# Local attention on one Trainium2 core: scores of even and odd heads in two PSUM banks, turned q and turned k in one

## The reference

```python
qkv = shift_tokens(x) @ Wqkv            # 128 -> 3 x 1024: 16 heads of 64
q = l2norm(q) * qs;  k = l2norm(k) * ksc
q = q * cos * scale + rotate_half(q) * sin * scale
k = k * cos / scale + rotate_half(k) * sin / scale
# windows of 32 queries; each sees its own and the previous 32 keys
sim = einsum('bhwie,bhwje->bhwij', bq, bk2) * 8.0
attn = softmax(where(mask, -big, sim))
x = einsum('bhwij,bhwje->bhwie', attn, bv2) @ Wo + x
x = (a * gelu(gate)) @ W2 + b2 + x      # a, gate from layernorm(shift_tokens(x)) @ W1 + b1
```

## Time and profile before

| | |
|---|---|
| median of 3 runs | 4349.73 us (4349.69 to 4349.89) |
| profiled execution, its own time | 4352.31 us |
| its span, first to last instruction | 4350.3 us |
| mean granted TensorE clock | 0.972 of full speed |
| the two local blocks, about | 365 to 1990 us and 2250 to 3870 us |
| a step without feed-forward work | 6.83 us |
| the step with the Gelu | 10.90 us |

### The profile page before, as it was taken

One profiled execution on the slowest core, in us unless ns is written; L12 is line 12 of the kernel. 1 busy time (PEld: TensorE's weight loads), 2 busy tenths in 40 slices (PEclk: granted clock), 3 DMA queues, 4 the chain that ended last, 5 costly groups with the idle time before them and its releaser, 6 DMA issues. The chain is left out here.

```text
span 4350.3 us, 128583 instructions
## 1 busy us (share of the span) xinstructions
PE 4059.4 (93%) x53847; PEld 2018.4 (46%) x53847; DVE 3351.9 (77%) x5020; ACT 2912.0 (67%) x7325; POOL 2388.5 (55%) x1684
## 2 busy tenths in 40 slices
PE   5998999999999999998989999999999999987897
PEld 3223555555455555553435555555554554543442
DVE  3776888888888888884758888888888888864673
ACT  2765777777777777774657777777777777754564
POOL 3314766666666666663226766666666666631220
PEclk7999999999999999997999999999999999999998
DMA  4221000000000000002220000000000000000110
GB/s 166 57 60 31 2 22 7 2 22 7 21 7 2 22 7 2 2 2 60 62 65 2 4 25 2 21 7 14 14 2 21 7 2 2 2 10 31 41 51 10
DMA packets 68917, 97.79 MB, mean 22 GB/s; under 512 B 34472, under 2 KB 58756, under 8 KB 62340
## 3 DMA queue, kind: packets, MB, share of 16 engines
q1 hardware_dynamic: 67476, 83.28, 6.5%
q10 hardware_dynamic: 864, 6.29, 0.4%
HBM read 72.18 MB, written 16.78 MB: 20 GB/s over the span
## 5 line engine op out<-in xcount | busy, mean ns | idle before, releaser
L402 POOL TENSOR_TENSOR ra<-ra,rb 128x1024 f32<-128x1024 f32 x384 | 927.2, 2415 | 330.2 <-DVE rb L741 330.1
L416 POOL TENSOR_TENSOR qkr<-ra,inv 128x1024 f32<-128x1024 f32 x384 | 731.0, 1904 | 608.2 <-ACT inv L680 604.5
L448 PE MATMUL ps<-wvo,xs 128*32 128x512 f32 x6144 | 821.2, 607 | 72.3 <-ACT vs L602 72.3
L493 PE MATMUL ps<-wq,xs 128*128 128x512 f32 x1536 | 747.8, 609 | 6.2 <-DVE rb L741 3.6
L653 ACT ACTIVATE pr<-ps,neg 128x64 f32<-128x64 f32 x3072 | 668.0, 337 | 7.1 <-DVE neg L718 7.1
L602 ACT ACTIVATE vs<-ps 128x512 f32<-128x512 f32 x768 | 450.8, 587 | 226.6 <-PE ps L448 225.3
L515 PEld LDWEIGHTS ps<-kt,qt 64*32 64x32 f32 x24576 | 360.3, 107 | 294.0 <-issue 290.3
L718 DVE TENSOR_REDUCE neg<-ps 128x8 f32<-128x512 f32 x384 | 263.7, 687 | 279.4 <-PE ps L515 272.5
L493 PEld LDWEIGHTS ps<-wq,xs 128*128 128x128 f32 x1536 | 274.0, 191 | 431.1 <-issue 334.0
L738 DVE TENSOR_TENSOR ra<-ps,rope 128x1024 f32<-128x1024 f32 x384 | 451.8, 1177 | 24.4 <-ACT sq L627 17.3
L1502 DVE TENSOR_REDUCE nm<-ps 128x1 f32<-128x512 f32 (+3 forms) x768 | 379.2, 550 | 116.9 <-PE ps L1267 114.4
(11 more groups left out here) (251 smaller groups left out, 6199.0 us busy)
## 6 DMA issues: line engine op xcount, KB each, us to landing
wq<-in_L_ffn_Wqkv SPq DMA_DIRECT2D x12, 1024.0 KB, 5.2
wvo<-wvo_scratch SPq DMA_DIRECT2D x12, 1024.0 KB, 4.9
wvo_scratch<-pt ACTq DMA_DIRECT2D x6, 1024.0 KB, 4.0
w<-in_L_ffn_W SPq DMA_DIRECT2D x12, 341.0 KB
qs<-norm_pieces SPq DMA_DIRECT2D x9, 384.0 KB
ks<-norm_pieces SPq DMA_DIRECT2D x9, 384.0 KB
qs<-latent_pieces SPq DMA_DIRECT2D x9, 384.0 KB
ks<-latent_pieces SPq DMA_DIRECT2D x9, 384.0 KB
```

What stands on the lines that cost most here:

```text
L402: pool.tensor_tensor(ra[:, m % 2, :, :], ra[:, m % 2, :, :], rb[:, :, :], ALU.add).then_inc(sum_done.sem, 1)
L416: pool.tensor_tensor(qkr[:, m % 2, :, :].rearrange("p s (h c) -> p (s h) c", c=HD), ra[:, m % 2, :, :].rearrange("p s (h c) -> p (s h) c", ...
L448: last = pe.matmul(VP[32 * j:32 * j + 32, :], xs[:, turn % 2, v * WIN:v * WIN + WIN], wvo[l % 2][:, j, :], start=True, stop=True)
L493: last = pe.matmul(PJ[:, qk, :], xs[:, turn % 2, t * P:t * P + P], wq[l % 2][:, at:at + 512], start=True, stop=True)
```

## The change

Four things change together.

1. Banks. SB becomes the first 256 columns of banks 3 and 4: even heads write bank 3, odd heads bank 4. Turned q and turned k share bank 2 (`TURN`). Eight consecutive products now use four strips of output partitions and both halves of the rows.
2. TensorE's order: turned q stands before the output product, turned k where both stood. Turned k waits for the copy of turned q, turned q for the copy of the previous turned k.
3. ScalarE copies turned q before the eight Exp. VectorE clamps the sum of squares before it copies turned k and adds the attention residual.
4. The heads come in another order within an item, and the preparation of the value weights (L1355 and the two copies behind it) follows.

The diff, without the lines that only rename indices in the preparation:

```diff
-    PJ, TQ, TK, SB, VP, PO, FB = ps[:, 0:2, :], ps[:, 2, :], ps[:, 3, :], ps[:, 4, :], ps[:, 5, :], ps[:, 6, :], ps[:, 7, :]
+    PJ, TURN, SB, VP, PO, FB = ps[:, 0:2, :], ps[:, 2, :], ps[:, 3:5, 0:TB * KEYS], ps[:, 5, :], ps[:, 6, :], ps[:, 7, :]
...
-                for i in range(2):
-                    for w in range(TB):
-                        for j in range(4):
-                            p, e = divmod(j, 2)
+                for w in range(TB):
+                    for pair in range(4):
+                        for e in range(2):
                             rows = slice(64 * e, 64 * e + 64)
-                            at = (i * TB + w) * KEYS
-                            last = pe.matmul(SB[32 * j:32 * j + 32, at:at + KEYS], qt[rows, m % 2, (2 * i + p) * TB + w, :],
-                                             kt[rows, 4 * up + 2 * i + p, t * P + w * WIN:t * P + w * WIN + KEYS], start=False, stop=i == 1 and w == TB - 1, skip_group_check=True)
+                            last = pe.matmul(SB[32 * pair:32 * pair + 32, e, w * KEYS:w * KEYS + KEYS], qt[rows, m % 2, pair * TB + w, :],
+                                             kt[rows, 4 * up + pair, t * P + w * WIN:t * P + w * WIN + KEYS], start=False, stop=w == TB - 1, skip_group_check=True)
...
+            m = item(k, LAG_TR)
+            if m is not None:
+                pe.wait_ge(qkr_done.sem, qkr_done.at(m + 1))
+                pe.wait_ge(k_kept.sem, k_kept.at(m))
+                for j in range(4):
+                    last = pe.transpose(TURN[:, j * P:j * P + P], qkr[:, m % 2, 0, j * P:j * P + P], core.ident[:, :])
+                last.then_inc(tq_ready.sem, 1)
             m = item(k, LAG_AV)
...
             m = item(k, LAG_TR)
             if m is not None:
-                pe.wait_ge(qkr_done.sem, qkr_done.at(m + 1))
-                pe.wait_ge(q_kept.sem, q_kept.at(m))
+                pe.wait_ge(q_kept.sem, q_kept.at(m + 1))
                 for j in range(4):
-                    last = pe.transpose(TQ[:, j * P:j * P + P], qkr[:, m % 2, 0, j * P:j * P + P], core.ident[:, :])
-                last.then_inc(tq_ready.sem, 1)
-                pe.wait_ge(k_kept.sem, k_kept.at(m))
-                for j in range(4):
-                    last = pe.transpose(TK[:, j * P:j * P + P], qkr[:, m % 2, 1, j * P:j * P + P], core.ident[:, :])
+                    last = pe.transpose(TURN[:, j * P:j * P + P], qkr[:, m % 2, 1, j * P:j * P + P], core.ident[:, :])
                 last.then_inc(tk_ready.sem, 1)
...
+            m = item(k, LAG_TR)
+            if m is not None:
+                act.wait_ge(tq_ready.sem, tq_ready.at(m + 1))
+                act.activation(qt[:, m % 2, :, :].rearrange("p w c -> p (w c)"), TURN, ACT.Copy).then_inc(q_kept.sem, 1)
             m = item(k, LAG_S)
...
-            m = item(k, LAG_TR)
-            if m is not None:
-                act.wait_ge(tq_ready.sem, tq_ready.at(m + 1))
-                act.activation(qt[:, m % 2, :, :].rearrange("p w c -> p (w c)"), TQ, ACT.Copy).then_inc(q_kept.sem, 1)
...
+            m = item(k, 0)
+            if m is not None:
+                dve.wait_ge(ss_done.sem, ss_done.at(m + 1))
+                dve.tensor_scalar(ssq[:, m % 2, :], ssq[:, m % 2, :], 1e-24, None, ALU.max).then_inc(ssc_done.sem, 1)
             m = item(k, LAG_TR)
             if m is not None:
                 dve.wait_ge(tk_ready.sem, tk_ready.at(m + 1))
...
-            m = item(k, 0)
-            if m is not None:
-                dve.wait_ge(ss_done.sem, ss_done.at(m + 1))
-                dve.tensor_scalar(ssq[:, m % 2, :], ssq[:, m % 2, :], 1e-24, None, ALU.max).then_inc(ssc_done.sem, 1)
```

More of the change, by code:

```diff
@@ L502, in tensor @@
                     pe.wait_ge(tables_done.sem, tables_done.at(1))
-                    pe.matmul(SB.rearrange("p (i c) -> p i c", i=2), core.ident16[:, :], band[:, None, :].to_broadcast([P, 2, TB * KEYS]),
-                              start=True, stop=False, skip_group_check=True)
+                    for e in range(2):
+                        pe.matmul(SB[:, e, :], core.ident16[:, :], band[:, :], start=True, stop=False, skip_group_check=True)
                 else:
@@ L652, in scalar @@
                 for n in range(8):
-                    last = act.activation(pr[:, m % 2, n, :], SB[:, n * KEYS:n * KEYS + KEYS], ACT.Exp, bias=neg[:, m % 2, n:n + 1])
+                    last = act.activation(pr[:, m % 2, n, :], SB[:, n // TB, n % TB * KEYS:n % TB * KEYS + KEYS], ACT.Exp, bias=neg[:, m % 2, n:n + 1])
                 last.then_inc(exp_done.sem, 1)
             before = m
-            m = item(k, LAG_TR)
-            if m is not None:
-                act.wait_ge(tq_ready.sem, tq_ready.at(m + 1))
-                act.activation(qt[:, m % 2, :, :].rearrange("p w c -> p (w c)"), TQ, ACT.Copy).then_inc(q_kept.sem, 1)
             if before is not None and before + 1 < STEPS:
@@ L662, in scalar @@
                 act.wait_ge(exp_done.sem, exp_done.at(before + 1))
-                act.activation(SB.rearrange("p (i c) -> p i c", i=2), bandf[:, kind, None, :].to_broadcast([P, 2, TB * KEYS]), ACT.Copy).then_inc(band_set.sem, 1)
+                act.activation(SB, bandf[:, kind, None, :].to_broadcast([P, 2, TB * KEYS]), ACT.Copy).then_inc(band_set.sem, 1)
             m = item(k, 0)
@@ L717, in vector @@
                 dve.wait_ge(s_ready.sem, s_ready.at(m + 1))
-                dve.tensor_reduce(neg[:, m % 2, :], SB.rearrange("p (n c) -> p n c", c=KEYS), AX.X, ALU.max, negate=True).then_inc(max_done.sem, 1)
+                dve.tensor_reduce(neg[:, m % 2, :].rearrange("p (e w) -> p e w", e=2), SB.rearrange("p e (w c) -> p e w c", c=KEYS), AX.X, ALU.max, negate=True).then_inc(max_done.sem, 1)
             m = item(k, LAG_PN)
@@ L771, in vector @@
                 t, up = divmod(m % STEPS_A_TURN, 2)
-                dve.tensor_copy(kt[:, 4 * up:4 * up + 4, WIN + t * P:WIN + t * P + P], TK.rearrange("p (k c) -> p k c", k=4)).then_inc(k_kept.sem, 1)
+                dve.tensor_copy(kt[:, 4 * up:4 * up + 4, WIN + t * P:WIN + t * P + P], TURN.rearrange("p (k c) -> p k c", k=4)).then_inc(k_kept.sem, 1)
             if (a := ff_turn(k, 3)) is not None:
@@ L984, in small_attention @@
         wvo = [pt[:, i, :].rearrange("p (j c) -> p j c", j=4) for i in range(2)]
+        by_unit = lambda a: a.rearrange("p j (u c) -> p u j c", u=4)
         wvt = [out[:, 2 * i:2 * i + 2, :].rearrange("p g (k c) -> p (g k) c", c=P) for i in range(2)]
@@ L1352, in tensor @@
                     for e in range(2):
-                        u, j = divmod(2 * c + e, 4)
+                        u, j = 2 * (c // 4) + e, c % 4
                         rows = slice(64 * e, 64 * e + 64)
-                        last = pe.matmul(ps[:, 2 + j, u * P:u * P + P], wvt[l % 2][rows, c, :], wo[l][rows, c, :], start=True, stop=True)
+                        last = pe.matmul(ps[:, 2 + u, j * P:j * P + P], wvt[l % 2][rows, c, :], wo[l][rows, c, :], start=True, stop=True)
                 last.then_inc(vw_mm.sem, 1)
@@ L1541, in vector @@
                     dve.wait_ge(vw_stored[l % 2].sem, vw_stored[l % 2].at(16 * (l // 2)))
-                dve.tensor_copy(wvo[l % 2][:, 2:4, :], ps[:, 4:6, :]).then_inc(vw_kept_dve.sem, 1)
+                dve.tensor_copy(by_unit(wvo[l % 2])[:, 2:4, :, :], ps[:, 4:6, :].rearrange("p u (j c) -> p u j c", j=4)).then_inc(vw_kept_dve.sem, 1)
             yield
```

2 lines of the change are left out of this document (1 added, 1 removed).

## The result

The changed kernel took 4493.95 us (median of 4 runs, 4491.43 to 4497.39) against 4349.81 for the kernel before in the same session: a ratio of 1.0324, 95% interval 1.0311 to 1.0336. The profiled execution spans 4495.4 us, 145 more than the 4350.3 of before. Of these 145, 142 lie in the two local blocks: counted from the first to the last score burst of each, they last 1595.9 and 1590.5 us before and 1666.5 and 1661.6 after.

A forecast was written before the change was run, and what follows sets the result against it. TensorE, busy 93%, was taken as the bound. Turns +87 us (46 of +1.90), first turns +6, tables +20, clock +17: +130 on 4350.3, 4480, less 2.6 about 4478 us; forecast 4430 to 4520 (0.58), range 4375 to 4560.

The forecast's parts named there:

- The score burst: TensorE's score products at each step's start: eight tiles at a time instead of four, a gain of 0.42 us.
- the mean step: Feed-forward step with the mean product, one per turn of eight steps: 0.42 us shorter, 7.60 us.
- the three other feed-forward steps: Feed-forward steps besides those with W2, mean product and Gelu: 0.14 us shorter each, 0.42 us a turn.
- the plain step: Step without feed-forward work: the next score burst waits for the k copy, 7.00 us instead of 6.83.
- Clamp, k copy, burst: VectorE's clamp held until GpSimd's addition ends, k copy behind it, next score burst waiting: plain step 7.00 us, not 6.69.
- Turned q and L416: TensorE's turned q waits for GpSimd's product: 0.70 us in the W2 step (10.40), 1.36 in the next (8.05).
- The Gelu step: Step where ScalarE computes the Gelu: turned k waits for the q copy, 11.70 us instead of 10.90.
- First turns and tables: Each block's first turn without feed-forward work, +6 us; ten times two table products delaying the k copy, +20 us.
- The clock: Ten more falls of the granted clock behind idle stretches of TensorE, 1.7 us each: +17 us.
- The faster rival: TensorE stays the bound, clamp not held or k copy on time, L416 ready: 4290 us, chance 0.13.
- No eight tiles: The score burst stays 1.03 us and only the costs stay: 4555 us, chance 0.10.
- part of what it says: Waits half as long as worked out, Gelu step as forecast: +0.9 us a turn, 4400 us, chance 0.15.

The follow-up runs named there:

- e1_clamp_alone: Kernel before, with only VectorE's clamp moved ahead of the copy of turned k: 4413.89 us, ratio 1.0133.
- e2_clamp_back: Changed kernel, with VectorE's clamp put back behind the k copy and the residual: 4502.51 us, ratio 1.0341.
- e7b_copy_late: Changed kernel, with GpSimd's two feed-forward copies moved behind its product L416: 4449.39 us, ratio 1.0221.
- f runs: ScalarE's first values copy moved ahead of the Gelu passes in three kernels: f1_between_gelu 4332.07 us, f2_before_gelu 4311.1 us, f3_after_gelu 4589.24 us.
- f3_after_gelu: Changed kernel, with ScalarE's copy of the first values product ahead of the Gelu passes: 4589.24 us, ratio 1.0539.
- g2_copy_gelu: f1_between_gelu, with ScalarE's q copy also ahead of the Gelu passes in the Gelu step: 4397.42 us, ratio 1.0089.
- f2_before_gelu: Kernel before, with ScalarE's copy of the first values product ahead of the Gelu passes: 4311.1 us, ratio 0.9906.
- g1_turn_gelu: f1_between_gelu, with the q copy ahead of the Gelu passes and turned q ahead of the output product, Gelu step only: 4318.63 us, ratio 0.9909.
- f1_between_gelu: e4_values_between, with ScalarE's copy of the first values product ahead of the Gelu passes: 4332.07 us, ratio 0.9952.
- e4_values_between: Changed kernel, TensorE order values, output product, turned q, second values, turned k, and the clamp behind the k copy: 4360.19 us, ratio 1.0012.

## Why the prediction was right, and where its sizes were off

The sign and the time were right (4478 forecast, 4494 measured), and so was the mechanism in each step that carried the sum. The total is 15 us short as a balance of larger errors: the turns cost 39 us more than forecast, the clock 25 less. That these offset each other is luck.

*The score burst* is the term that was mis-sized. From its start to the first values it takes 0.79 us (1284.45 to 1285.24), not 0.61: a gain of 0.24 instead of 0.42. Eight tiles do run together, but not to the end of the burst. The passes of the burst that touch each quarter of a microsecond (count in brackets, PE then PEld; a pass that crosses a border counts twice), in the changed kernel and in the kernel before:

```profile
1284.45:1284.70 0.25, 0.25 (x32) 0.25 (x33) 1.00 0.00 0
1284.70:1284.95 0.25, 0.25 (x48) 0.25 (x29) 1.00 0.00 0
1284.95:1285.20 0.25, 0.25 (x31) 0.20 (x22) 1.00 0.00 0
```

```profile
1244.96:1245.21 0.25, 0.25 (x17) 0.25 (x20) 1.00 0.00 0
1245.21:1245.46 0.25, 0.25 (x34) 0.25 (x27) 1.00 0.00 0
```

32 passes in the first quarter against 17. By their starts, the first 32 come in groups of eight, a group every 56 ns with 6.7 ns from pass to pass inside it; before, they come in groups of four every 56 ns. The other 32 are about 12 ns apart on average. Why the groups of eight end after 32 passes, no run shows. The prediction had named this risk ("64 passes must also be issued in half the time") and gave it 0.02 us; it was 0.18. It recurs in the mean step, which gains 0.24 us instead of 0.42, and in the three other feed-forward steps, which each lose 0.05 instead of gaining 0.14: 0.76 us a turn, 35 us in all. It is also the larger part of what the plain step is longer than forecast (7.14 for 7.00: maximum at 0.90 instead of 0.75). That maximum also moves the whole chain behind it.

*Clamp, k copy, burst.* The chain was right: clamp held to within 0.03 us of the end of the addition, copy, burst. The burst begins 0.15 us after the end of the k copy, where 0.07 was taken. e1_clamp_alone confirms the cause by itself at 58 us. What the prediction did not say, and e2_clamp_back shows, is that in the changed kernel the clamp costs nothing that turned q would not cost too: with the clamp back, the plain step and the one behind W2 lose 0.11 and 0.20 us, and the W2 step gains 0.48 as a longer wait for L416.

*Turned q and L416.* Forecast as waits of 0.70 and 1.36 us in the W2 step and the one behind it; measured 0.38 and 1.14. TensorE arrives 0.18 later by the longer burst (1.79 us after its start, not 1.61); the product ends at 2.17 instead of 2.24 in the first and at 2.94 instead of 2.90 in the second. The third wait, 0.36 us in the Gelu step, was not forecast. So the total of 96.9 us, near the 95 that two waits in each of 46 turns would give, agrees by luck: the two forecast ones make 70. The steps themselves came out at 10.34 (10.40) and 8.09 (8.05). e7b_copy_late confirms the cause of the second.

*The Gelu step:* 11.68 for 11.70; the wait stands at the k transposes, for the q copy, as forecast. The f runs show that the wait there hangs on the shared bank and on where ScalarE frees it. No run gave turned q and turned k a bank each beside the new score layout, so what sharing costs by itself was not measured.

*First turns and tables:* +5 for +6, and about +16 for +20. In each of the ten table turns one step is now 8.8 us where others have 7.8 (10 us) and one 8.1, before 7.8, where others have 7.7 (2.5 us); twelve steps of other turns are 8.05 instead of 7.79 (3 us).

*The clock:* forecast +17, measured about -8. Before, 4 of 44 Gelu steps took 13.15 us with a stretch at the lower clock, and six 11.5; after, three took 13.3. Some 6 of the 8 us are not the clock: the longer waits of the ten table turns, 0.6 us each, are gone. I had set the new waits of about 1.6 us near the 1.98 of the earlier trace rows. The 34 waits of 1.54 lost no clock; in the ten table turns, for which I had taken 2.1, the wait is 1.76 and three lost it.

Together: 39 us more from the turns, 25 less from the clock, 5 less from first turns and tables, and 6 more elsewhere, half of them outside the two blocks: 145 in place of 130. The faster rival fell on the clamp and L416, as its own condition said. "No eight tiles" was nearly half true in size: the burst gained 0.24 of the 0.42. The rival "part of what it says" has a slip: +0.9 a turn with the other +43 of the sum is 4432, not 4400, and lies inside the forecast's own range.

## What to carry over

Before an operation is moved, see what it is waiting on where it stands, and what will stand behind it where it goes: a 16-column operation cost 58 us by holding a copy. When two buffers become one, look at the step in which the engine that empties it is away longest, here ScalarE in its Gelu passes, and not at the mean step; whatever frees TensorE's next bank belongs ahead of such a stretch. But each operation put there delays what TensorE needs from the stretch itself and from behind it, which cost more than it gave in f3_after_gelu and g2_copy_gelu. That rule, applied to the unchanged kernel by moving one copy, gave the fastest version of this study (f2_before_gelu, 4311 us, 0.9906), and the change's own score layout, with another order of TensorE and two copies moved, reached the same (g1_turn_gelu, 4319 us, 0.9909) but not more.

## What the runs showed of the hardware

- Passes of 64 rows by 32 columns into two banks start in groups of eight every 56 ns, where those of the kernel before start in groups of four every 56 ns, but in a burst of 64 this holds only for the first 32, 7.7 ns from start to start on average; from there it is about 12 ns.
- Of the 44 Gelu steps behind the first turns, by their longest wait of TensorE, so many lost the granted clock (0.50 for some 3 us, 1.6 us or more lost): none with 0.67 us, in one 1.02 (f2_before_gelu), none with 1.11, in ten 1.3 (g1_turn_gelu), none with 1.37 (e1_clamp_alone), 22 with 2.16 (f1_between_gelu), 33 with 2.44 to 2.66 (f3_after_gelu), 30 with 2.47 to 2.67 (e4_values_between), 29 with 2.85, in one 3.20 (g2_copy_gelu). In the kernel before, none of the 34 waits of 1.37 us but four of the ten of 1.98. In the changed one the idle time of all 44 steps adds up to 1.90 us: of the 34 with 0.36 and 1.54 none lost the clock, of the ten with 0.14 and 1.76 three did. In g1_turn_gelu 1.89 us in two pieces, and 2.08 in the ten, kept it. So the longest piece tells more than the sum; but those ten are the table turns in each kernel, and no run varied the piece alone.
- The change of tile shape costs 0.12 us on TensorE each time, and the plain step of e4_values_between, which was computed with it, came out as computed (6.55).
- The Trainium skill (TensorEngine Tiling (Array Packing), Restrictions and Gotchas) says that different row tiles cannot access the same bank simultaneously. The burst of the kernel before does not fit this as it stands: its groups of four, 6.7 ns from start to start, hold passes of both row halves that all write the one bank SB. They write different strips of partitions. No run here put eight tiles into one bank, so what that would do was not tried.
